# Writing the bf16 high parts of q and k with ScalarE and cutting the rests by halves in both self-attention layers

## What is computed

```python
# layer 0: causal self-attention over 77 context keys and 1024 own keys, then an MLP
q, k, v = split(layernorm(x) @ w_qkv + b_qkv); ck, cv = split(context @ w_ckv + b_ckv)
x = x + softmax(q @ concat(ck, k).T / 4, causal) @ concat(cv, v); x = x + gelu(ln(x) @ w1) @ w2
# layer 1: linear attention to the context and a window of 64 tokens on the own keys
q = rmsnorm(x) @ Wq; k, v = split(context @ Wkv); kw, vw = split(rmsnorm(x) @ Wwin)
linear = phi(q @ Wqf) @ (phi(k @ Wkf).T @ v) / normalizer
window = softmax(q @ kw.T / 4, 0 <= i - j <= 64) @ vw
x = x + concat(linear, window) @ Wout
# layers 2 and 3: cross-attention to the context (masked and weighted, then plain)
```

## Time and profile before

| | |
|---|---|
| median of 3 runs | 2310.28 us (2308.71 to 2311.33) |
| the profiled execution | 2313.2 us, its span from the first to the last instruction 2311.5 us |
| mean granted TensorE clock | 0.955 |
| busy of the span | PE 2053.5 us (89%), DVE 1409.0 (61%), ACT 1112.0 (48%), POOL 739.2 (32%) |
| L913 causal copies, L915 window copies | 22.0 + 2.6 us, 21.1 us of ACT |
| L1040 casts to high parts | 15.8 us (causal), 11.4 us (window) of DVE |
| L1050 casts to middle parts | 15.5 us, 24.1 us of DVE |
| L1044 rests of batch 0 | 6.9 us, 5.1 us of DVE |

### The profile page before, as it was taken

The page is one execution under the profiler, slowest core; times in us unless marked ns, Lnnn a source line. Parts: engine busy times, 40 slices in busy tenths (PEclk is TensorE's granted clock), DMA queues, the critical chain, the costliest instruction groups (busy, mean ns, idle before and its releaser), DMA issues. The chain is left out here.

```text
span 2311.5 us, 38268 instructions
## 1 busy us (share of the span) xinstructions
PE 2053.5 (89%) x14610; PEld 1348.9 (58%) x14610; DVE 1409.0 (61%) x3047; ACT 1112.0 (48%) x1675; POOL 739.2 (32%) x858
## 2 busy tenths in 40 slices
PE   4998999999898879997889898898989996999989
PEld 2333433343343268875565475566677775888989
DVE  5875786686668366645536355352577884756654
ACT  1264464555454766533434534344455554545444
POOL 2023114113213243412524515243301101555656
PEclk8799999999999989998999899899999998999999
DMA  6705404502530000028440714520422210000000
GB/s 145 132 6 109 58 1 79 92 2 50 93 73 1 1 15 1 10 74 108 108 64 30 127 17 94 79 81 1 145 93 83 83 56 1 8 13 12 15 12 20
DMA packets 77771, 126.66 MB, mean 55 GB/s; under 512 B 16650, under 2 KB 34826, under 8 KB 77582
## 3 DMA queue, kind: packets, MB, share of 16 engines
q1 hardware_dynamic: 74966, 122.63, 25.6%
q10 hardware_dynamic: 2624, 1.58, 0.2%
HBM read 93.59 MB, written 30.32 MB: 54 GB/s over the span
## 5 line engine op out<-in xcount | busy, mean ns | idle before, releaser
L1056 DVE TENSOR_REDUCE nmx_causal<-banks 128x1 f32<-128x333 f32 (+4 forms) x896 | 435.1, 538 | 166.3 <-PE banks L786 164.2
L940 ACT ACTIVATE probs_causal<-banks 128x1024 f32<-128x1024 f32 (+5 forms) x384 | 331.0, 898 | 292.3 <-PE banks L811 288.7
L786 PE MATMUL banks<-ks_causal,qs_causal 96*128 96x333 bf16 (+4 forms) x896 | 273.5, 341 | 13.6 <-DVE nmx_causal L1056 11.6
L709 POOL TENSOR_SCALAR_AFFINE_SELECT probs_causal<-probs_causal 128x512 f32<-128x512 f32 (+2 forms) x160 | 97.8, 612 | 514.4 <-ACT probs_causal L940 514.1
L709 POOL TENSOR_SCALAR_AFFINE_SELECT probs_window<-probs_window 128x512 f32<-128x512 f32 (+1 forms) x272 | 162.9, 605 | 309.3 <-ACT probs_window L940 298.8
L811 PE MATMUL banks<-qs_causal,ks_causal 97*128 97x512 bf16 (+5 forms) x896 | 211.5, 332 | 27.5 <-ACT probs_causal L940 14.7
L1056 DVE TENSOR_REDUCE nmx_window<-banks 128x2 f32<-128x384 f32 (+2 forms) x320 | 140.8, 459 | 109.3 <-PE banks L786 107.6
L835 PE MATMUL banks<-probs_causal,v_causal 128*17 128x512 f32 (+5 forms) x1792 | 187.0, 490 | 0.0
L940 ACT ACTIVATE probs_window<-banks 128x768 f32<-128x768 f32 (+2 forms) x128 | 99.9, 783 | 127.0 <-PE banks L811 126.3
L786 PEld LDWEIGHTS banks<-ks_causal,qs_causal 96*128 96x128 bf16 x896 | 87.0, 100 | 111.6 <-DVE nmx_causal L1056 72.6
L784 PEld LDWEIGHTS banks<-below,identb 128*128 128x128 bf16 x512 | 50.2, 99 | 171.2 <-DVE nmx_causal L1056 113.6
(11 more groups left out here) (255 smaller groups left out, 4121.4 us busy)
## 6 DMA issues: line engine op xcount, KB each, us to landing
fs_masked<-in_fside SPq DMA_DIRECT2D x32, 616.0 KB, 3.7
ks_causal<-zk SPq DMA_DIRECT2D x96, 137.6 KB
ks_window<-zk SPq DMA_DIRECT2D x96, 137.6 KB
qs_causal<-zq SPq DMA_DIRECT2D x96, 128.0 KB
qs_window<-zq SPq DMA_DIRECT2D x96, 128.0 KB
zk<-parts_causal SPq DMA_DIRECT2D x24, 275.2 KB, 2.5
zk<-parts_window SPq DMA_DIRECT2D x24, 275.2 KB, 2.4
zq<-parts_causal SPq DMA_DIRECT2D x24, 256.0 KB, 8.5
```

What stands on the lines that cost most here:

```text
L709: pool.affine_select(out=v, in_=v, compare_op=ALU.is_ge, fill=0.0, base=const, pattern=[[0, QH], [by_c, wd]], channel_multiplier=by_p).the ...
L786: ins = pe.matmul(bk[:, c:c + m], qs[q][0:KR, h, t * P:(t + 1) * P], ks[q][0:KR, h, key:key + m], start=cover is None, stop=True, skip_gro ...
L940: ins = act.activation(dst, src, ACT.Exp, scale=DH ** -0.5)
L1056: dve.tensor_reduce(dst, src, AX.X, ALU.max, negate=True).then_inc(emptied_v, 1)
```

## The change

ACT now reads each bank of `kc` and `qk` twice: once for the bf16 high part (`parts[:, u % 2, 0]`), and once for `whole`. The `high` token is gone; a `rest` token and a `middle` token stand for each half of a unit (589 columns for the first half of k, else 512). `rest` is the subtraction (DVE in batch 0, POOL later), `middle` the cast on DVE and the low part on POOL. SP still writes whole units, at the token of the second half. The write of the high part has a semaphore of its own, `high_written`, for which ACT waits before it fills the slot again. The list of a batch's projection grows from 42 to 50 tokens in the window layer and from 40 to 48 in the causal one. The helper `ring` and the bank counts are as before.

```diff
     for u in range(4):
         if u % 2 == 0:
             tokens.append(("kc", b, u))
-        tokens += [("qk", b, u, 0), ("qk", b, u, 1), ("high", b, u)]
-        if u >= lag:
-            tokens.append(("middle", b, u - lag))
-    return tokens + [("middle", b, u) for u in range(4 - lag, 4)]
+        for half in range(2):
+            tokens += [("qk", b, u, half), ("rest", b, u, half)]
+            if u >= lag:
+                tokens.append(("middle", b, u - lag, half))
+    return tokens + [("middle", b, u, half) for u in range(4 - lag, 4) for half in range(2)]
...
-                batch.insert(1 + max(batch.index(("middle", b + 1, q // 2 * 2 + 1)), last_of(q)), ("stack", b + 1, q))
+                batch.insert(1 + max(batch.index(("middle", b + 1, q // 2 * 2 + 1, 1)), last_of(q)), ("stack", b + 1, q))
...
+    def part_of(u, half):
+
+        if units[u][0]:
+            return slice(half * BANK, (half + 1) * BANK)
+        return slice(half * (S + BANK), S + (half + 1) * BANK)
...
-            elif what == "high":
-                write(*args, 0, high)
-            elif what == "middle":
-                write(*args, 1, middle)
-                write(*args, 2, low)
+            elif what == "rest" and args[2]:
+                write(*args[:2], 0, high, 1)
+            elif what == "middle" and args[2]:
+                write(*args[:2], 1, middle, 2)
+                write(*args[:2], 2, low, 2)
...
-                pool.tensor_tensor(out, whole[:, u % 2, 0:n], parts[:, u % 2, part, 0:n],
-                                   ALU.subtract).then_inc(low if part else rest, 1)
+                b, u, half = args
+                cols = part_of(u, half)
+                if what == "rest":
+                    pool.wait_ge(*ring.emptied(("qk", b, u, half)))
+                    pool.tensor_tensor(whole[:, u % 2, cols], whole[:, u % 2, cols], parts[:, u % 2, 0, cols],
+                                       ALU.subtract).then_inc(rest, 1)
+                else:
+                    pool.wait_ge(middle, 2 * unit_number[b, u] + half + 1)
                     half_done(pool, b, u)
+                    pool.tensor_tensor(parts[:, u % 2, 2, cols], whole[:, u % 2, cols], parts[:, u % 2, 1, cols],
+                                       ALU.subtract).then_inc(low, 1)
...
-                    act.wait_ge(low, unit_number[b, u] - 1)
+                    act.wait_ge(low, 2 * (unit_number[b, u] - 1))
+                    act.wait_ge(high_written[u % 2], high_before(b, u))
...
-                if first:
-                    ins = act.activation(dst, src, ACT.Identity, bias=bias[0][:, bias[1]:bias[1] + 1])
-                else:
-                    ins = act.activation(dst, src, ACT.Copy)
+
+                for dst in (parts[:, u % 2, 0, cols], whole[:, u % 2, cols]):
+                    if first:
+                        ins = act.activation(dst, src, ACT.Identity, bias=bias[0][:, bias[1]:bias[1] + 1])
+                    else:
+                        ins = act.activation(dst, src, ACT.Copy)
+                    if dst.dtype == BF16 and what == "qk" and args[2]:
+                        ins.then_inc(high, 1)
                 ins.then_inc(emptied_s, 1)
...
-                dve.tensor_copy(parts[:, u % 2, 0, 0:n], whole[:, u % 2, 0:n]).then_inc(high, 1)
-                if b == 0:
-
-                    dve.wait_ge(high, unit_number[b, u] + 1)
-                    dve.tensor_tensor(whole[:, u % 2, 0:n], whole[:, u % 2, 0:n],
-                                      parts[:, u % 2, 0, 0:n], ALU.subtract).then_inc(rest, 1)
...
+            elif what == "middle":
+                b, u, half = args
+                cols = part_of(u, half)
+                dve.wait_ge(rest, 2 * unit_number[b, u] + half + 1)
                 half_done(dve, b, u)
-                dve.tensor_copy(parts[:, u % 2, 1, 0:n], whole[:, u % 2, 0:n]).then_inc(middle, 1)
+                dve.tensor_copy(parts[:, u % 2, 1, cols], whole[:, u % 2, cols]).then_inc(middle, 1)
```

More of the change, by code:

```diff
@@ L178, in attention_tokens @@
         order.append(token)
-        if token in (("middle", 0, 1), ("middle", 0, 3)):
+        if token in (("middle", 0, 1, 1), ("middle", 0, 3, 1)):
             order += [("stack", 0, token[2] - 1), ("stack", 0, token[2])]
-    order += [("rest",)] if first else []
+    order += [("x_rest",)] if first else []
     head, order = order, ring_tokens(0, 0, ring_jobs) + [("shift", 0, 0)]
@@ L528, in attention_layer @@
     ring_ready, emptied_v, emptied_s = ring.ready, ring.ring.done["v"], ring.ring.done["s"]
-    written = [sem("written0"), sem("written1")]
+    high_written, written = ([sem(f"{s}{n}") for n in range(2)] for s in ("high_written", "written"))
     shift_loaded = [sem("shift_loaded0"), sem("shift_loaded1")]
@@ L560, in sync, with write @@
     def sync(sp):
-        def write(b, u, part, cut):
+        def write(b, u, part, cut, count):
             is_q, m = units[u]
-            sp.wait_ge(cut, unit_number[b, u] + 1)
+            sp.wait_ge(cut, count * (unit_number[b, u] + 1))
             n = T if is_q else KW
             sp.dma_start((zq if is_q else zk)[b, part, m * P:(m + 1) * P, :],
-                         parts[:, u % 2, part, 0:n]).then_inc(written[u % 2], 16)
+                         parts[:, u % 2, part, 0:n]).then_inc((written if part else high_written)[u % 2], 16)
         def step(token):
@@ L630, in finish @@
                 sp.wait_ge(stacked[q], 16 * (12 * B + 1))
-            for done in written:
-                sp.wait_ge(done, writes_before(B, 0))
+            for n in range(2):
+                sp.wait_ge(high_written[n], high_before(B, 0))
+                sp.wait_ge(written[n], writes_before(B, 0))
             if not first:
@@ L686, in step @@
                 pool.tensor_copy(pad[:, 1, :, S:P], xnT[:, :, 0:P - S]).then_inc(padded, 1)
[L687 to L694 removed]
+            if what == "middle" or what == "rest" and args[0]:
+                b, u, half = args
[6 more added lines that the diff above has]
+                    pool.wait_ge(middle, 2 * unit_number[b, u] + half + 1)
                     half_done(pool, b, u)
[L696 to L697 removed]
+                    pool.tensor_tensor(parts[:, u % 2, 2, cols], whole[:, u % 2, cols], parts[:, u % 2, 1, cols],
+                                       ALU.subtract).then_inc(low, 1)
             elif what == "scores":
```

40 lines of the change are left out of this document (16 added, 24 removed).

## The result

The changed kernel takes 2277.68 us (median of four runs, 2266.12 to 2284.93) beside 2309.49 us of the kernel before in the same session. The ratio is 0.9865, with a 95% interval from 0.9833 to 0.9897: about 31 us faster. The profiled execution took 2284.93 us, 28.3 less than that of before.

The account below looks back on a forecast made before the run. PE was taken to pace both attention layers, other engines costing time only where PE waits. Terms -4.1 - 2.7 - 8.0 - 3.0 - 15 + 7 = -25.8 us gave 2287.4 us profiled, 2284.5 median; range 2272 to 2305.

Parts of the forecast that it names:

- the main case: Whole kernel: PE's stops at heads, shifts, maxima and window projections shrink or go; 2284.5 us by the median, chance 0.48.
- Causal head: Start of the causal layer: unit 1's low part ready at 31.3 against 35.38; gain 4.1 us, bounds 3.0 and 5.0.
- Its own sign of being wrong: DVE's casts: the forecast is wrong if casts of 512 columns take 1 us or more each.
- Window head: Start of the window layer: low part ends at 1029.7 against 1032.41; gain 2.7 us, bounds 1 and 4.
- Shift transfers of the causal layer: Causal main part: backlog drains 4 to 8 us sooner; gain 8.0 of 9.9 us of PE waits, bounds 0 and 9.9.
- The sign given for it: Causal layer: L811's three waits for the shift's DMA gone or at most 1 us, its landing at 2 us.
- Ring maxima: Causal main part: shorter DVE casts cut PE's 6.3 us of waits behind maxima; gain 3 us, bounds 0 and 6.3.
- Window main part: Window layer's projections: four PE stops a batch mostly go, 5.0 us in each of three batches; gain 15, bounds 0 and 20.4.
- ACT's second write: Batches 1 to 3: ring banks are free 0.69 us later, PE and exps wait; loss 7 us, bounds 2 and 34.
- The transfers do not give their part back: Rival, causal shift: landing depends on transfers in flight, not backlog age, so three waits stay; 2292.5 us, chance 0.17.
- Only the heads return: Rival, main parts: every removed stop is met by a new one at the ring banks; 2303.5 us, chance 0.23.
- ACT keeps the banks: Rival, ring banks: PE pays the full 34 us of second writes, third window stop stays; 2318 us, chance 0.07.

Follow-up runs that it names:

- `halves_only`: Changed kernel with work still by halves, but DVE casts the high part again and ACT writes each bank once: 2273.04 us, ratio 0.9857.
- `high_only`: Changed kernel with ACT's two writes kept, but rests, middle casts and low parts in whole units and the shorter list: 2312.54 us, ratio 1.0027.
- `stacks_wait`: Changed kernel with next-batch stack loads moved behind the fourth shift, SP also waiting until that shift's transfer has landed: 2258.99 us, ratio 0.9796.
- `third_write`: Changed kernel with ACT writing the bf16 high part twice, so each projection bank is held for three activations: 2309.43 us, ratio 0.9990.

## Why the prediction was right, and where its steps were off

The forecast was 2284.5 us with a range from 2272 to 2305; 2277.68 was measured. The direction and the mechanism of the main case, whole stops of PE that go away as the work is cut in halves, held. Its terms:

- **Causal head, -4.1:** -2.8 at PE's start and -2.0 at the stack's issue, both short of the lower bound, a gain of 3.0. The step that failed is the one that took a cast at 0.37 us and a POOL half at 1.07 between 27.71 and 31.3: beside each other they take 1.27 and 1.69. The bound of 3.0 had one such meeting in it, of 1.07 us; the forecast had none. The prediction took up the shared port in the window layer only, while it is the head that had several meetings in a row. Its own sign of being wrong, casts of 512 columns at 1 us or more, came true for 12 of the 64 casts of halves. The load took 13.8 us instead of 14.6, which gave the other 0.8.
- **Window head, -2.7:** the wait fell from 9.27 to 5.84, -3.4. Right.
- **Shift transfers of the causal layer, -8.0:** the waits from 150 to 620 fell from 9.9 to 1.0, those from 60 to 650 from 12.1 to 3.2. Right in size. The sign given for it was not: the landing was to be 2 us and was 4.4 to 6.0. The wait is gone since the transfer lands just in time. The backlog became 4 to 5 us older (its last transfer is issued 12.2 to 13.8 us before the shift's, and not 8.3 to 8.8); that the list's order gave 3.6 of them, as the prediction has it, no run tests.
- **Ring maxima, -3:** the line of the earlier trace rows fell from 6.3 to 3.2, as forecast. But it is one of several: all waits of PE behind ring maxima from 150 to 620 sum to 10.3 us before and 8.9 after, so the term was mis-sized, 3 us where 1.4 came.
- **Window main part, -15:** from the first to the last shift 506.0 us became 489.4, -16.6, with the second write and 2.9 us of longer shift waits in it. All four kinds of stop are gone, and the clock of the projection is 1.00. Somewhat undersized. Not foreseen was the fourth shift: the prediction asked after it only in the causal layer. Its transfer ran beside the stacks in the window layer too, issued 24 to 11 us ahead of it before and 22 to 8 now; it landed in 2.4 to 6.0 us before and in 3.4 to 8.0 now.
- **ACT's second write, +7:** 5.5 us of waits behind the copies in the causal layer, where there had been 1.7, and 2.0 in the window layer: some 6 us more, near the size given. But `halves_only`, without them, is no faster. What they cost the time stays open: `halves_only` against the changed kernel is 0.9857 to 0.9865, each known to some 8 us, and `high_only`, with the second write and no halves, is some 6 us slower than the kernel before. A cost of 7 is neither shown nor excluded.

Together the sum was -25.8 for a profiled execution; by the medians it is -31.8, and up to the window layer's last shift the trace has -36.9. With the write's 7 us shared out evenly, the window main part is -16.6 against -11.5, the causal main part -12.1 against -7.5, and the MLP with the window head -5.4 against -2.7. For the window layer the runs show what the terms left out, that a stop also costs clock behind it (`stacks_wait`); that it holds in the causal layer too is only argued, and the 2 us that the MLP gave beside the head's wait are not explained. 8.6 us were then lost in untouched layers, so the profiled execution's 2284.93 lies near the 2287.4 forecast for it by a chance of its clock.

**The rivals.** "The transfers do not give their part back" is refuted for the waits; the landing itself did stay long, 4.4 to 6.0 us. The rule that the prediction cites for it from the Trainium skill (DMA: Bandwidth & Descriptors, "Queues, rings and completion order"), that each DMA engine takes turns between queues packet by packet, would make the landing the same however old the backlog is, as long as some is there. Here it went from 6.3 us with a backlog issued 8 to 22 us before to 11.7 with one issued in the 12 us before. How much data was still under way in each case the traces do not show, so the rule itself is not tested; the runs show only that the small transfer is not safe beside a backlog. "Only the heads return" is refuted by the lead of 12.1 us in the causal layer behind its head. "ACT keeps the banks" is refuted at two writes, and `third_write` shows that it is a real mechanism one write further.

What the change was made of mattered more than the prediction said. It gave no weight to which edit pays; the runs give all of it to the halves, short pieces and denser list together.

## What to carry to other kernels

When one engine's long instructions sit in another engine's queue, cutting them in two can pay without taking any work away; look for waits that are as long as such an instruction. Here the longer list that comes with them is part of the same gain, and what each gives is open. Before taking work off an engine with idle time, ask who waits for it: DVE lost all its high casts here, 15.8 + 11.4 us, to a second write of ACT, and alone that gave nothing (`high_only`). And order small urgent transfers against bulk ones by a wait, not by the place in the list: moving the stacks in the list alone put 24 bulk transfers right in front of the small one (1.0022 against 0.9865, 36 us lost), and one wait in the same place made it 0.9796, 16 us won.

## What the runs showed of the hardware

- **A cast of DVE waits for POOL's instruction to end.** In the changed kernel's timeline POOL's 1.54 us from 29.75 end at 31.29, and the cast, begun at 30.30, ends at 31.57, 0.28 later. Of its 64 middle casts 31 began while POOL was in a subtraction or a mask; all 31 ended 0.28 to 0.32 us behind that instruction, and in the kernel before so did all 26 of the 64 high and middle casts that began beside POOL, at 0.55 to 0.60 us for 1024 or 1101 columns. The rest beside the same POOL instruction, at 29.59, keeps its 0.68 us, but POOL, begun at 29.75, ends 1.02 us after the rest does, at 30.27. POOL waits in turn: all six of its low parts that began while a rest of DVE ran ended 0.95 to 1.09 us behind that rest, and the three rests that began while POOL ran ended 0.55 us behind POOL. The Trainium skill, SBUF — State Buffer, "SBUF: two separate sides", has this as an exclusive lock of the shared port pair, for DVE instructions in a two-port mode or with two SBUF inputs, and the trace agrees in both directions.
- **Stops of 2.8 and 4.6 us cost 7 and 6.** The granted clock of the stretch with and behind them was 0.81 and 0.84, not 0.93 and 0.96. Directly behind the first it was 0.52 and 0.50 for 8 us, the lower of the two levels (1.2 and 2.4 GHz), and behind the second 0.50 from 1417 to 1421.
- **ACT writes bf16 as fast as float32.** 512 columns from a bank took 689 ns in bf16 and 682 in float32 (mean of 32 each), so the bf16 form brings nothing for ACT.
